# Table slices in PSUM as operands of VectorE's products, and the second power made in halves

## The chip, the cores and the metric

The kernel runs on one core of a Trainium2 chip. The metric is the device time of one execution in microseconds, the median of three runs. An execution has five engines at work beside each other: TensorE (PE in the profile), VectorE (DVE), ScalarE (ACT), GpSimd (POOL) and SyncE (SP), which issues the transfers here. Semaphores order them.

## What is computed

A state space kernel gives the tokens, and a transformer layer follows (attention of 32 heads with a causal mask, and a gated feed-forward part with quantised weights). Only the first stage, the state space kernel and the layer norm behind it, is touched by the change:

```
dt = exp(log_dt); A = -exp(inv_A_real) + 1j * A_imag          # (H=128, N=64)
dtA = A * dt[:, None]
Cc = (B * C) * (exp(dtA) - 1) / A                             # (16, 128, 64)
V = exp(dtA[:, :, None] * arange(1024))                       # (128, 64, 1024)
h = 2 * einsum('chn,hnl->chl', Cc, V).real                    # (16, 128, 1024)
h = h + attention(layernorm(h)); h = h + ffn(layernorm(h))
```

## The kernel before

`ssm_and_norm` makes h and its layer norm. The power exp(dtA l) is never made for all l at once: l is written as 128 i + 16 j + m (i and j below 8, m below 16), and small tables hold the powers of each part, `tab1` for the real part and `tab2` for the imaginary part (with rows 64 to 127 of the partitions arranged for the other component), 32 entries a channel. Columns 0 to 7 of a channel (i) go, rotated by the coefficients, into `a1` and `a2`; columns 8 to 15 (j) and 16 to 31 (m) are multiplied out to the 128 powers of a channel.

The 128 channels go in 16 units (`UNITS`) of 8 channels (`UH`). For a unit u:

- GpSimd multiplies `tab1` slices out to `v` (L238), then `a1` by `c_re` to the first factor `w[s][0]` (L241), then channels 0 to 2 (`CUT` is 3) of `a2` by `c_im` (L242).
- VectorE makes channels 3 to 7 of that last product (`second_factor`, L459), multiplies the `tab2` slices out to `v_second`, a tile of two PSUM banks (`second_power`, L465), and adds it to `v` (`power`, L469).
- TensorE multiplies `v` by the two factors, four channels to a half (`product(u, 0)` and `product(u, 1)`, L258), and ScalarE brings each half out (`columns`, L315). TensorE transposes it to tokens (`to_tokens`, L267), ScalarE copies them out with their total (`tokens`, L323) and SP writes them to the chip's memory (L168).
- The layer norm follows: VectorE's `mean` (L475), ScalarE's `squares` (L331) and `deviation` (L336), VectorE's `inverse` (L481), ScalarE's `normalise` (L340, L342), TensorE's `to_features` (L275), ScalarE's `high` (L346) and VectorE's `low` (L485).

`v`, `w`, `tok` and `nrm` have two buffers each, `v_second`, `pt` and `pn` one. Every engine runs a loop over k that is written out by hand and takes the steps of different units in a fixed order; `each(lag, k)` says whether unit k - lag exists. VectorE's turn k is: second_factor(k + 1), inverse(k - 2), second_power(k + 1), power(k + 1), low(k - 3), then in turns 1 to 6 one step of `rotations` of the second half of the channels, in turns 7 to 10 a quarter of the search for the largest of the next stage's first weights (L650), in turn 13 `find_scale` (L658 and on), mean(k - 1), and in turns 14 and 15 `first.low`. ScalarE's turn is high(k - 3), normalise(k - 2), columns(k, 0), tokens(k - 1), columns(k, 1), squares(k - 1), deviation(k - 1), and in turns 13 and 14 `first.high`. TensorE's is product(k, 0), to_tokens(k - 1), product(k, 1), to_features(k - 2). Behind the token write of unit 10 SP sends the largest weight out and back to all partitions (`exchange`: two small transfers, wv_bigs and wv_all, the second waits for the first). A barrier of all engines ends the stage.

The semaphore `s_v` counts the units whose power is done; `s_mm` counts halves of products; `s_wd`, `s_wp` and `s_v1` say that VectorE's factor, GpSimd's factors and GpSimd's power are ready.

Of the kernel before, what the change touches and what calls it, by code (L numbers as in the profile page):

```python
# [15 lines left out]
P = 128  # L16
# [69 lines left out]
def ssm_and_norm(nc, ssm, cr, ci, h0_dram, xn_hi, xn_lo, ident, w_first, wv_first, b_first, first, rooms):  # L86
# [9 lines left out]
    with ExitStack() as st:  # L96
# [31 lines left out]
        with ExitStack() as tables_only:  # L128
            phase_ps = [tables_only.enter_context(nc.psum_tensor(f"phase_ps{k}", [P, HALF_H, TAB], F32)) for k in two]
        ps = [st.enter_context(nc.psum_tensor(f"ssm_ps{s}", [P, UH // 2, P], F32)) for s in two]  # L130
        v_second = st.enter_context(nc.psum_tensor("v_second", [P, UH * P], F32))
# [6 lines left out]
        s_v1, s_v, s_wp, s_wd, s_mm, s_tr, s_tok, s_mean, s_sq, s_std, s_rs, s_nrm, s_trn, s_hi, s_lo = (  # L138
            sem("a_" + n) for n in ("v1", "v", "wp", "wd", "mm", "tr", "tok", "mean", "sq", "std", "rs", "nrm", "trn", "hi", "lo"))
# [106 lines left out]
        def _(pe):  # L246
            def product(u, part):
                s = u % 2
                if part == 0:
                    pe.wait_ge(s_v, u + 1)  # L250
                    pe.wait_ge(s_wp, u + 1)
                    pe.wait_ge(s_wd, u + 1)
                if u:
                    pe.wait_ge(s_ev[part], u)
                for h in range(UH // 2):
                    cols = slice((part * UH // 2 + h) * P, (part * UH // 2 + h + 1) * P)
                    for k in two:
                        last = nc.tensor.matmul(ps[part][:, h, :], v[s][:, cols], w[s][k][:, cols], start=(k == 0), stop=(k == 1))  # L258
                last.then_inc(s_mm, 1)
# [29 lines left out]
        def _(act):  # L289
# [59 lines left out]
            for k in range(UNITS + 3):  # L349
                if k == UNITS:  # L350
                    tokens(k - 1)
                if each(3, k):
                    high(k - 3)
                if each(2, k):
                    normalise(k - 2)
                if each(0, k):
                    columns(k, 0)
                if each(1, k) and k < UNITS:
                    tokens(k - 1)
                if each(0, k):  # L360
                    columns(k, 1)
                if each(1, k):
                    squares(k - 1)
                    deviation(k - 1)
                if k in (UNITS - 3, UNITS - 2):
                    act.wait_ge(s_v, UNITS // 2)
                    first.high(nc, act, 0, k - UNITS + 3)

        @block.vector
        def _(dve):  # L370
# [83 lines left out]

            def second_factor(u):
                s, hs = u % 2, channels(u, CUT, UH)
                if u >= 2:
                    dve.wait_ge(s_mm, 2 * (u - 1))
                tt(four(w[s][1], C)[:, CUT:UH], bc(a2[:, hs, :], C, 3), bc(cim[:, hs, :], KT, 2), ALU.mult).then_inc(s_wd, 1)  # L459

            def second_power(u):
                ch = channels(u)
                if u:
                    dve.wait_ge(s_v, u)
                chain.after(tt(four(v_second[:], TJ), bc(tab2[:, ch, TI:2 * TI], TJ, 3), bc(tab2[:, ch, 2 * TI:TAB], TI, 2), ALU.mult))  # L465

            def power(u):
                dve.wait_ge(s_v1, u + 1)
                tt(v[u % 2], v[u % 2], v_second[:], ALU.add).then_inc(s_v, 1)  # L469
# [17 lines left out]

            for k in range(-1, UNITS + 3):
                if each(-1, k):
                    second_factor(k + 1)  # L490
                if each(2, k):
                    inverse(k - 2)
                if each(-1, k):
                    second_power(k + 1)
                    power(k + 1)
                if each(3, k):
                    low(k - 3)
                if 1 <= k < 7:
                    rotations(1, k - 1)
                if 7 <= k < 11:  # L500
                    first.find_big_quarter(nc, dve, chain, 0, k - 7)
                if k == UNITS - 3:
                    first.find_scale(nc, dve, chain, 0)
                if each(1, k):
# [2165 lines left out]
```

## Time and profile before

| | |
|---|---|
| median of 3 runs | 1905.37 us (1904.93 to 1909.08) |
| profiled execution | 1913.66 us, span 1911.9 us |
| TensorE, busy share of the span | 93% (1787.0 us) |
| VectorE | 70% (1335.3 us) |
| GpSimd | 52% (992.7 us) |
| ScalarE | 39% (749.7 us) |
| granted TensorE clock, mean | 0.990 |

The profile is one execution of its own, and its times are compared with its own span. In its rows a line number is that of the kernel above, an arrow leads from what is read to what is written, x16 is a count, and a time in brackets is how long the engine stood idle before it, with what released it. Tiles that lie in the room of others go by the name of the room: `v` is shown as magnitude, `w` as phase, `tab1` as w_qk and `tab2` as w_v.

### The profile page before, as it was taken

How to read it: one execution, taken by the hardware profiler on the slowest of the kernel's cores; microseconds unless marked ns; L12 is line 12 of the kernel's file. 1: busy time of each engine (PE TensorE's matmuls, PEld its weight loads, DVE VectorE, ACT ScalarE, POOL GpSimd, SP SyncE). 2: the span in 40 equal slices, each digit the busy share in tenths (PEclk: the TensorE clock that was granted, in tenths of full speed). 3: DMA queues.
4: the chain of work that ended last, by engine and by line, in shares of the span. 5: the costliest groups of instructions: out<-in, count | busy, mean ns of one | idle time of the engine just before them, and what ended most of it. 6: DMA issues, size and time to landing. Idle time of an engine off the chain costs nothing.

```text
span 1911.9 us, 31551 instructions
## 1 busy us (share of the span) xinstructions
PE 1787.0 (93%) x12772; PEld 975.9 (51%) x12772; DVE 1335.3 (70%) x1695; ACT 749.7 (39%) x1072; POOL 992.7 (52%) x675
## 2 busy tenths in 40 slices
PE   0577899999999999999999999999999999999999
PEld 0576566666666656554555344444444444444444
DVE  8996477877788888865555877775665555367775
ACT  4478143433434345431212554544544443112221
POOL 6973043433434333442261366765577776377672
PEclk9998899999999999999999999999999999999999
DMA  2122202111021221126541333333455453533531
GB/s 98 36 75 68 61 15 60 40 37 39 18 88 62 62 75 62 34 99 225 168 138 64 103 113 118 117 115 119 157 155 195 150 170 121 198 131 117 193 114 67
DMA packets 102704, 194.92 MB, mean 102 GB/s; under 512 B 14304, under 2 KB 75488, under 8 KB 92064
## 3 DMA queue, kind: packets, MB, share of 16 engines
q1 hardware_dynamic: 102560, 192.90, 31.4%
q8 instruction: 102, 1.67, 0.4%
q14 instruction: 42, 0.34, 0.1%
HBM read 135.72 MB, written 56.11 MB: 100 GB/s over the span
## 4 chain that ended last, share of the span: by engine, by line
PE 74%; DVE 9%; POOL 2%; issue 2%; ACT 2%; DMA 1%; SPq 0%; DVEq 0%; ACTq 0%
PE acc L1481 13%; PE acc L1483 12%; PE acc L1649 9%; PE acc L1614 4%; PE ps_p L1273 4%; PE ps_p L1275 4%; PE ps_p L1274 4%; PE ps_t L1300 3%; PE acc L1387 3%; PE acc L1388 3%; PE acc L1389 3%; PE ps_p L1289 2%; PE ps_p L1291 2%; PE ps_p L1290 2%; PE ps_l L1490 2%
## 5 line engine op out<-in xcount | busy, mean ns | idle before, releaser
L1127 POOL TENSOR_TENSOR prob<-prob,mx 128x1024 f32<-128x1024 f32 x64 | 121.4, 1897 | 379.8 <-DVE mx L2078 379.8
L1273 PE MATMUL ps_p<-x_hi,w_qk 128*128 128x512 f16 x512 | 194.7, 380 | 0.0
L1274 PE MATMUL ps_p<-x_lo,w_qk 128*128 128x512 f16 x512 | 194.0, 379 | 0.0
L1275 PE MATMUL ps_p<-x_hi,w_qk 128*128 128x512 f16 x512 | 194.0, 379 | 0.0
L1180 POOL TENSOR_TENSOR hidden<-up,hidden 128x512 f16<-128x512 f32 x80 | 91.0, 1159 | 144.3 <-ACT hidden L1907 144.0
L1289 PE MATMUL ps_p<-w_v,x_hi 128*128 128x256 f16 x512 | 142.3, 278 | 7.2 <-PEq L825 3.6
L1132 POOL TENSOR_TENSOR prob<-prob,sm 128x1024 f32<-128x1024 f32 x64 | 120.1, 1896 | 52.9 <-DVE sm L2085 52.9
L1290 PE MATMUL ps_p<-w_v,x_hi 128*128 128x256 f16 x512 | 142.2, 278 | 0.0
L1291 PE MATMUL ps_p<-w_v,x_lo 128*128 128x256 f16 x512 | 142.2, 278 | 0.0
L1741 ACT ACTIVATE pth<-ps_t 128x512 f16<-128x512 f32 x128 | 76.1, 595 | 163.7 <-PE ps_t L1300 163.7
L2330 DVE SCALAR_TENSOR_TENSOR up<-acc,gu_scale,up 128x512 f32<-128x512 f32 x120 | 90.0, 750 | 61.1 <-PE acc L1483 60.0
L258 PE MATMUL ssm_ps<-phase,magnitude 128*128 128x128 f32 x512 | 69.1, 294 | 65.3 <-DVE magnitude L469 62.1
L2330 DVE SCALAR_TENSOR_TENSOR gate<-acc,gu_scale,gate 128x512 f32<-128x512 f32 x120 | 89.7, 747 | 56.2 <-PE acc L1483 55.4
L1481 PE MATMUL acc<-x_hi,q_sums 128*128 128x512 f16 x320 | 121.7, 380 | 1.1 <-issue 0.8
L1481 PE MATMUL acc<-x_sum,q_sums 128*128 128x512 f16 x320 | 121.3, 379 | 0.0
L1483 PE MATMUL acc<-x_sum,q_sums 128*128 128x512 f16 x320 | 121.3, 379 | 0.0
L1483 PE MATMUL acc<-x_lo,q_f 128*128 128x512 f16 x320 | 121.3, 379 | 0.0
L1481 PE MATMUL acc<-x_hi,q_f 128*128 128x512 f16 x320 | 121.3, 379 | 0.0
L1483 PE MATMUL acc<-x_lo,q_sums 128*128 128x512 f16 x320 | 121.3, 379 | 0.0
L2089 DVE SCALAR_TENSOR_TENSOR ptl<-ps_t,pth 128x512 f16<-128x512 f32 x128 | 87.7, 685 | 47.3 <-ACT pth L1741 46.8
L1899 ACT ACTIVATE gate<-gate 128x512 f32<-128x512 f32 (+1 forms) x88 | 55.1, 626 | 135.8 <-DVE gate L2330 133.2
L258 PEld LDWEIGHTS ssm_ps<-phase,magnitude 128*128 128x128 f32 x512 | 66.1, 209 | 65.8 <-DVE magnitude L469 62.3
(386 smaller groups left out, 4598.0 us busy)
## 6 DMA issues: line engine op xcount, KB each, us to landing
q_raw<-in_gu_q SPq DMA_DIRECT2D x42, 1024.0 KB, 6.3
hid_parts<-hidden_parts SPq DMA_DIRECT2D x16, 1376.0 KB, 6.8
hidden_parts<-hidden SPq DMA_DIRECT2D x42, 512.0 KB, 3.5
down_raw<-in_down_q SPq DMA_DIRECT2D x22, 512.0 KB, 3.6
w_raw<-in_w_qk SPq DMA_DIRECT2D x8, 1024.0 KB, 4.8
h_tokens<-n_tok SPq DMA_DIRECT2D x16, 512.0 KB, 3.7
o_parts<-ot SPq DMA_DIRECT2D x32, 256.0 KB, 2.3
wv_raw<-in_w_o SPq DMA_DIRECT2D x8, 1024.0 KB, 4.9
```

The costliest lines, as they stand in the source:

```text
L258: last = nc.tensor.matmul(ps[part][:, h, :], v[s][:, cols], w[s][k][:, cols], start=(k == 0), stop=(k == 1))
L1127: nc.gpsimd.tensor_tensor(prob[s % 2][p][:], prob[s % 2][p][:], bc(mx[p][:], H, 2), ALU.subtract).then_inc(s_sub[p], 1)
L1273: nc.tensor.matmul(out[:], w[:, j % 2, m, 0, at], xn_hi[:, k, tok], start=(k == 0), stop=False)
L1274: nc.tensor.matmul(out[:], w[:, j % 2, m, 0, at], xn_lo[:, k, tok], start=False, stop=False)
L1275: last = nc.tensor.matmul(out[:], w[:, j % 2, m, 1, at], xn_hi[:, k, tok], start=False, stop=(k == KT - 1))
L1289: nc.tensor.matmul(out, xn_hi[:, k, tok], wv[:, g % 2, 0, at], start=(k == 0), stop=False)
L1290: nc.tensor.matmul(out, xn_hi[:, k, tok], wv[:, g % 2, 1, at], start=False, stop=False)
L1291: last = nc.tensor.matmul(out, xn_lo[:, k, tok], wv[:, g % 2, 0, at], start=False, stop=(k == KT - 1))
L1481: nc.tensor.matmul(banks[bank], lev[:, k * P:(k + 1) * P], hi[:, k, :], start=(k == 0 and not adds), stop=False, skip_group_check=adds)
L1483: last = nc.tensor.matmul(banks[bank], lev[:, k * P:(k + 1) * P], lo[:, k, :], start=False, stop=(k == KH - 1), skip_group_check=adds)
L1649: last = nc.tensor.matmul(banks[bank], of_hid(i, part), of_levels(i), start=(not adds and i == 0 and part == 0), stop=(ends and i == KD - ...
L2330: stt(to[:], banks[bank], scl[:, m, i:i + 1], to[:], ALU.mult, ALU.add).then_inc(s_read, 1)
```

## The change

A new PSUM tile `cuts` holds, for two units, the `tab2` slice of columns 8 to 15 of all eight channels and the `a2` slice of channels 3 to 7. The new `slices(u)` copies both with two TENSOR_SCALAR calls (times 1.0) on VectorE, for unit 0 ahead of the loop and for unit k + 2 in turn k. `second_factor` and `second_power` read these copies in place of the tables in SBUF. `second_power` and `power` are made in two parts of four channels, and `v_second` is half as large, so that one bank serves both parts. VectorE's turn k is now: second_factor(k + 1), second_power(k + 1, 0), inverse(k - 2), power(k + 1, 0), low(k - 3), second_power(k + 1, 1), the rotation, slices(k + 2), the quarter or find_scale, power(k + 1, 1), mean(k - 1). `s_v` counts parts, and TensorE waits for the part that it multiplies. The other inputs of the two products (`cim` and columns 16 to 31 of `tab2`) stay in SBUF, as do all operands of GpSimd.

```diff
--- before.py
+++ after.py
@@ -128,15 +128,16 @@
         with ExitStack() as tables_only:
             phase_ps = [tables_only.enter_context(nc.psum_tensor(f"phase_ps{k}", [P, HALF_H, TAB], F32)) for k in two]
         ps = [st.enter_context(nc.psum_tensor(f"ssm_ps{s}", [P, UH // 2, P], F32)) for s in two]
-        v_second = st.enter_context(nc.psum_tensor("v_second", [P, UH * P], F32))
+        v_second = st.enter_context(nc.psum_tensor("v_second", [P, UH // 2 * P], F32))
+        cuts = st.enter_context(nc.psum_tensor("cuts", [P, 2, 2 * UH, TI], F32))
         pt = st.enter_context(nc.psum_tensor("n_pt", [P, KT, P], F32))
         pn = st.enter_context(nc.psum_tensor("n_pn", [P, KT, P], F32))
 
         s_in, s_c, s_const, s_dve, s_re, s_im, s_expm, s_square, s_pool, s_ab, s_turn = (
             sem("a_" + n) for n in ("in", "c", "const", "dve", "re", "im", "expm", "square", "pool", "ab", "turn"))
         s_mag, s_phase, s_trig, s_tab, s_a = (sem("a_" + n) for n in ("mag", "phase", "trig", "tab", "a"))
-        s_v1, s_v, s_wp, s_wd, s_mm, s_tr, s_tok, s_mean, s_sq, s_std, s_rs, s_nrm, s_trn, s_hi, s_lo = (
-            sem("a_" + n) for n in ("v1", "v", "wp", "wd", "mm", "tr", "tok", "mean", "sq", "std", "rs", "nrm", "trn", "hi", "lo"))
+        s_v1, s_v, s_wp, s_wd, s_mm, s_tr, s_tok, s_mean, s_sq, s_std, s_rs, s_nrm, s_trn, s_hi, s_lo, s_cut = (
+            sem("a_" + n) for n in ("v1", "v", "wp", "wd", "mm", "tr", "tok", "mean", "sq", "std", "rs", "nrm", "trn", "hi", "lo", "cut"))
         s_out, s_ev = ([sem(f"a_{n}{s}") for s in two] for n in ("out", "ev"))
         logdt, inva, aim, br, bi = (par[:, k, :] for k in range(5))
         nc.all_engine_barrier()
@@ -246,8 +247,8 @@
         def _(pe):
             def product(u, part):
                 s = u % 2
+                pe.wait_ge(s_v, 2 * u + part + 1)
                 if part == 0:
-                    pe.wait_ge(s_v, u + 1)
                     pe.wait_ge(s_wp, u + 1)
                     pe.wait_ge(s_wd, u + 1)
                 if u:
@@ -363,7 +364,7 @@
                     squares(k - 1)
                     deviation(k - 1)
                 if k in (UNITS - 3, UNITS - 2):
-                    act.wait_ge(s_v, UNITS // 2)
+                    act.wait_ge(s_v, UNITS)
                     first.high(nc, act, 0, k - UNITS + 3)
 
         @block.vector
@@ -452,21 +453,38 @@
             dve.wait_ge(s_tab, 2)
             dve.wait_ge(s_c, 32)
 
+            def slices(u):
+
+                s, ch, hs = u % 2, channels(u), channels(u, CUT, UH)
+                if u >= 2:
+                    dve.wait_ge(s_v, 2 * (u - 1))
+                    dve.wait_ge(s_wd, u - 1)
+                ts(cuts[:, s, 0:UH, :], tab2[:, ch, TI:2 * TI], 1.0, None, ALU.mult).then_inc(s_cut, 1)
+                ts(cuts[:, s, UH + CUT:2 * UH, :], a2[:, hs, :], 1.0, None, ALU.mult).then_inc(s_cut, 1)
+
             def second_factor(u):
                 s, hs = u % 2, channels(u, CUT, UH)
+                dve.wait_ge(s_cut, 2 * (u + 1))
                 if u >= 2:
                     dve.wait_ge(s_mm, 2 * (u - 1))
-                tt(four(w[s][1], C)[:, CUT:UH], bc(a2[:, hs, :], C, 3), bc(cim[:, hs, :], KT, 2), ALU.mult).then_inc(s_wd, 1)
-
-            def second_power(u):
-                ch = channels(u)
-                if u:
-                    dve.wait_ge(s_v, u)
-                chain.after(tt(four(v_second[:], TJ), bc(tab2[:, ch, TI:2 * TI], TJ, 3), bc(tab2[:, ch, 2 * TI:TAB], TI, 2), ALU.mult))
-
-            def power(u):
+                tt(four(w[s][1], C)[:, CUT:UH], bc(cuts[:, s, UH + CUT:2 * UH, :], C, 3), bc(cim[:, hs, :], KT, 2),
+                   ALU.mult).then_inc(s_wd, 1)
+
+            def second_power(u, part):
+
+                mine = slice(part * UH // 2, (part + 1) * UH // 2)
+                ch = channels(u, part * UH // 2, (part + 1) * UH // 2)
+                if u or part:
+                    dve.wait_ge(s_v, 2 * u + part)
+                return chain.mark(tt(v_second[:].rearrange("p (h a b) -> p h a b", h=UH // 2, b=TJ), bc(cuts[:, u % 2, mine, :], TJ, 3),
+                                     bc(tab2[:, ch, 2 * TI:TAB], TI, 2), ALU.mult))
+
+            def power(u, part, made):
+
+                cols = slice(part * UH // 2 * P, (part + 1) * UH // 2 * P)
                 dve.wait_ge(s_v1, u + 1)
-                tt(v[u % 2], v[u % 2], v_second[:], ALU.add).then_inc(s_v, 1)
+                dve.wait_ge(s_dve, made)
+                tt(v[u % 2][:, cols], v[u % 2][:, cols], v_second[:], ALU.add).then_inc(s_v, 1)
 
             def mean(u):
                 dve.wait_ge(s_tok, u + 1)
@@ -485,22 +503,29 @@
                 tt(xn_lo[:].rearrange("p k (c h) -> p k c h", h=H)[:, :, :, channels(u)], pn[:].rearrange("p k (c h) -> p k c h", h=UH),
                    xn_hi[:].rearrange("p k (c h) -> p k c h", h=H)[:, :, :, channels(u)], ALU.subtract).then_inc(s_lo, 1)
 
+            slices(0)
             for k in range(-1, UNITS + 3):
                 if each(-1, k):
                     second_factor(k + 1)
+                    made = second_power(k + 1, 0)
                 if each(2, k):
                     inverse(k - 2)
                 if each(-1, k):
-                    second_power(k + 1)
-                    power(k + 1)
+                    power(k + 1, 0, made)
                 if each(3, k):
                     low(k - 3)
+                if each(-1, k):
+                    made = second_power(k + 1, 1)
                 if 1 <= k < 7:
                     rotations(1, k - 1)
+                if each(-2, k):
+                    slices(k + 2)
                 if 7 <= k < 11:
                     first.find_big_quarter(nc, dve, chain, 0, k - 7)
                 if k == UNITS - 3:
                     first.find_scale(nc, dve, chain, 0)
+                if each(-1, k):
+                    power(k + 1, 1, made)
                 if each(1, k):
                     mean(k - 1)
                 if k in (UNITS - 2, UNITS - 1):
```

## Rows read from the trace of the kernel before

**Rows 1.** Chain that ended last, from its start: start us, us, what.
```profile
194.30 2.30 DVE w_big L2040
```

**Rows 2.** Timeline, VectorE's means of units 0, 5, 11, 14: start us, us, engine, line.
```profile
74.16 0.14 DVE L475 TENSOR_SCALAR n_mean<-n_total 128x1 f32<-128x1 f32 x1
...
111.67 0.15 DVE L475 TENSOR_SCALAR n_mean<-n_total 128x1 f32<-128x1 f32 x1
...
154.38 0.15 DVE L475 TENSOR_SCALAR n_mean<-n_total 128x1 f32<-128x1 f32 x1 [0.63 <-ACT n_tok L323]
...
177.87 0.15 DVE L475 TENSOR_SCALAR n_mean<-n_total 128x1 f32<-128x1 f32 x1 [2.88 <-ACT n_tok L323]
```

**Rows 3.** Grouped lines of VectorE, first stage from 57 us: busy us, mean ns.
```profile
L465 DVE TENSOR_TENSOR v_second<-w_v 128x1024 f32<-128x1024 f32 x16 | 34.3, 2142 | 0.0
L459 DVE TENSOR_TENSOR phase<-a,c_im 128x640 f32<-128x640 f32 x16 | 27.7, 1728 | 0.6 <-PE ssm_ps L258 0.5
```

**Rows 4.** Single lines: shortest, median and longest of one (ns), first and last start.
```profile
L459 DVE TENSOR_TENSOR phase<-a,c_im x16: 816/1926/2581, 57.1 to 163.3; 128x640 f32<-128x640 f32 x16
...
L465 DVE TENSOR_TENSOR v_second<-w_v x16: 1215/1842/2962, 57.8 to 165.8; 128x1024 f32<-128x1024 f32 x16
...
L469 DVE TENSOR_TENSOR magnitude<-magnitude,v_second x16: 1220/1221/1222, 60.8 to 167.6; 128x1024 f32<-128x1024 f32 x16
...
L241 POOL TENSOR_TENSOR phase<-a,c_re x16: 1920/2510/2930, 57.1 to 163.2; 128x1024 f32<-128x1024 f32 x16
```

**Rows 5.** Timeline, VectorE beside GpSimd (POOL), 96 to 99 us.
```profile
96.09 2.38 POOL L241 TENSOR_TENSOR phase<-a,c_re 128x1024 f32<-128x1024 f32 x1
...
96.61 0.14 DVE L475 TENSOR_SCALAR n_mean<-n_total 128x1 f32<-128x1 f32 x1
96.67 2.48 DVE L459 TENSOR_TENSOR phase<-a,c_im 128x640 f32<-128x640 f32 x1
```

**Rows 6.** Timeline of ScalarE, one unit from 127 us; idle time in brackets.
```profile
127.08 1.15 ACT L331 ACTIVATE magnitude<-n_tok,n_mean 128x1024 f32<-128x1024 f32 x1 [1.85 <-DVE n_mean L475]
...
128.56 1.00 ACT L346 ACTIVATE x_hi<-n_pn 128x1024 f16<-128x1024 f32 x1
...
132.40 0.59 ACT L315 ACTIVATE n_xt<-ssm_ps 128x512 f32<-128x512 f32 x1
```

**Rows 7.** Timeline of TensorE, half of a product.
```profile
127.31 1.95 PE L258 MATMUL ssm_ps<-phase,magnitude 128*128 128x128 f32 x16
```

**Rows 8.** Grouped lines of VectorE before 57 us, shapes kept apart.
```profile
L404 DVE TENSOR_SCALAR w_qk<-phase_ps 128x2048 f32<-128x2048 f32 x2 | 4.6, 2291 | 0.1
...
L381 DVE TENSOR_SCALAR n_nrm<-ssm_par 128x256 f32<-128x256 f32 x1 | 0.3, 294 | 1.2 <-DMA ssm_par<-in_ssm 1.2
```

**Rows 9.** Timeline, first unit of the loop, all engines.
```profile
57.11 2.56 POOL L241 TENSOR_TENSOR phase<-a,c_re 128x1024 f32<-128x1024 f32 x1 [3.48 <-DVE a L443]
...
59.63 1.82 POOL L242 TENSOR_TENSOR phase<-a,c_im 128x384 f32<-128x384 f32 x1
...
62.07 1.22 PE L258 MATMUL ssm_ps<-phase,magnitude 128*128 128x128 f32 x4 [62.07 <-DVE magnitude L469]
```

**Rows 10.** Timeline around the exchange of the largest weight, all engines and SP's queue.
```profile
146.49 0.20 ACT L323 ACTIVATION_READ_ACCUMULATOR n_tok<-n_pt 128x1 f32 x1
...
147.28 0.59 SPq L628 DMA_DIRECT2D wv_bigs<-wv_big  x1
...
155.79 0.33 SPq L630 DMA_DIRECT2D wv_all<-wv_bigs  x1
...
161.04 0.28 DVE L658 TENSOR_REDUCE wv_pow<-wv_all 128x1 f32<-128x128 f32 x1
...
161.28 1.92 POOL L238 TENSOR_TENSOR magnitude<-w_qk 128x1024 f32<-128x1024 f32 x1
...
162.12 1.11 DVE L660 TENSOR_SCALAR bv_scaled<-b_qkv,wv_scale 128x2 f32<-128x2 f32 x1
```

**Rows 11.** DMA issues, 60 to 200 us: count, KB each, median us to landing.
```profile
wv_all<-wv_bigs SPq DMA_DIRECT2D x1, 64.0 KB, 4.5
```

## The prediction

> **What bounds the kernel now.** I read the page's shares first (TensorE is busy 93% of the span, but the stage around the change is the first tenth), then the chain of work that ended last, from its beginning. The chain opens at 194 us with the reduction of the next stage's weights [rows 1]: it stands behind the barrier that ends the first stage and waits for nothing that has a clock of its own. So whatever the first stage ends earlier, the kernel ends earlier by the same amount. Next I read the timeline of the first stage, unit by unit. VectorE's `mean` (L475) occurs once in a unit: from unit 0 at 74.16 to unit 14 at 177.87 [rows 2] are 14 periods, 7.41 us each. What fills a period? The grouped lines give `second_factor` (L459) a mean of 1728 ns and `second_power` (L465) 2142 ns [rows 3]; one operation's own spread gives their shortest as 816 and 1215 ns, while `power` (L469), of the same 1024 elements as L465 but with one operand in PSUM, never left 1220 to 1222 ns [rows 4]. The reader is to see that spread: the same work takes up to 2962 ns. The timeline of VectorE beside GpSimd shows why: L459 starts at 96.67, while GpSimd works from 96.09 to 98.47, and ends at 99.15, 0.68 us after GpSimd's end, which is the time that its 640 elements take [rows 5]. With both operands in SBUF, whoever comes second stands still until the other is done. The excess over the shortest is 0.91 us and 0.93 us a unit, 29.4 us over 16 units [rows 3, 4]. ScalarE sees it as waits for the mean, as the 1.85 us before its square at 127.08 [rows 6].
>
> **What the stage can fall to.** ScalarE's work of one unit goes from the square at 127.08 to `columns` at 132.40, 5.32 us, plus about 0.5 for that last copy: 5.8 us a unit without the waits [rows 6]. TensorE needs less: two halves of a product of 1.95 [rows 7] and two sets of eight transposes, half as many instructions, by that estimate 1.0 each: 5.9, near ScalarE's; the layout below looks at whether the two collide. GpSimd needs 1.92 twice and, for 384 elements at the same rate, 0.83: 4.6 us [rows 4] (the 0.83 is 384 elements at 1.75 to 1.85 ns with some 0.15 fixed, an estimate from L241's shortest, 1920 ns for 1024). So ScalarE is late next, not VectorE's blocked products.
>
> **Price of each part.** From 816 ns for 640 elements and 1220 for 1024 [rows 4] VectorE pays 1.05 ns an element and 0.15 a call; neighbours that wait for nothing start 0.08 before the end of the one in front (96.67 is before 96.61 + 0.14) [rows 5]. (1) `second_factor` reads its table operand from `cuts` in PSUM: 1.73 becomes 0.82, a step of 0.75. (2) `second_power` in halves of 512: 0.68 each, step 0.61, so 1.22 for 2.14. (3) `power` in halves: 1.22 for a step of 1.14, plus 0.08. In the other order the wait of power for second_power goes behind `inverse`, the rotation or the copies. (4) `slices`: two calls of 64 and 40 elements that no row shows. Nearest are a TENSOR_SCALAR of 256 elements from SBUF to SBUF at 294 ns, and 2048 elements out of PSUM at 2291 ns [rows 8]: 0.15 is the lower end; the upper end is 0.2 plus one whole GpSimd operation of 1.92, because L660, a TENSOR_SCALAR of 2 elements, took 1.11 us from 162.12 to 163.23, when the GpSimd operation of 161.28 ended [rows 10]. I take 0.2 each, 0.25 in steps for both: 256 elements in 294 ns are half a nanosecond each, two a cycle, and that form could be what blocked; 2048 out of PSUM run at 1.05 ns, so an operand in PSUM gives up the double rate, and `cuts` is one. (5) The waits on s_cut, s_v and s_wd name work that VectorE finished before in its own order; they cost nothing while that order holds. Were a copy late, `inverse`, the products and `low` would stand behind `second_factor` on VectorE, and ScalarE's `normalise` would wait for them; the copies are made a whole unit ahead, so five other VectorE steps lie between. (6) TensorE's wait moves from the whole power to its half: product(u, 0) may start one half earlier, which no engine waits for once ScalarE is the bound. (7) One bank less for v_second and one for the copies: no time, unless a PSUM operand read with repeats is slower. Lower bound 1.05 ns an element as in L469, upper twice that; I take the lower, as L465's repeats out of SBUF cost nothing in its shortest run [rows 4].
>
> The Trainium skill, page SBUF — State Buffer, section Who interferes with whom, says that `tensor_scalar` can take the two-port mode and then is fully blocked by GpSimd; this speaks against the copies, and would make each cost as much as the upper end; by that rule L660 agrees [rows 10]. Its page VectorE: DVE Perf Modes, section Mode 2×_2P, says that this mode requires SBUF, which would leave them at 0.2; the two rates agree [rows 8]. No row of before has the mixed form, SBUF in and PSUM out.
>
> **One period laid out**, with the mean at 0. ScalarE squares at 0.2, starts `high` at 1.7 and ends it at 2.7 (128.56 is 1.48 after 127.08, for 1.0) [rows 6]. VectorE: factor and first half done by 1.45, `inverse` at 1.8 behind the deviation (ScalarE's call in front of `high`), first power to 2.5, `low` from 2.7 on, its 1024 elements a step of 1.14, to 3.85, second half to 4.45, copies to 4.7, power to 5.3: mean possible at 5.3, but ScalarE's total is there only at 5.6 (`columns` starts 5.32 behind the square) and its next square follows at 6.0, so the period is 5.8. TensorE: `to_features` from the end of `normalise` at 4.1, product(k + 1, 0) to 7.0, the transposes to tokens, product(k + 1, 1) to 9.7, which is 3.7 of the next period; `columns` of the first half is wanted at 10.0, three after its product. TensorE holds up nobody, and starts GpSimd's next unit at 3.7. With a rotation or a quarter of the maximum (0.7) the mean comes at 6.0: period 6.0. A rotation still has two SBUF operands and meets GpSimd's first product of that unit: it is held up to 1.1 us in one period and less in the next, 0.5 on the mean: 6.5.
>
> **The sum.** Head: GpSimd's operations of 2.56 and 1.82 at 57.11 and 59.63 [rows 9] become 1.92 and 0.83, ready at 59.9; VectorE has copied and made its half by 59.6; the first product starts at 60.0, not 62.07 [rows 9]. Unit 1 is then GpSimd's 4.6 later, 64.5 (first part 59.9 + 1.9, and so on); unit 2's first power waits for GpSimd at 66.3, and behind it come a half, a rotation held to 68.7, the copies and a power: mean(0) at 69.7, not 74.16: −4.4. Means 0 to 5, with rotations: 6.5 each for 37.5 now: −5.0. Means 5 to 11: four with quarters at 6.0, 0.4 for what follows the last of them, two at 5.8, against 42.7: −6.6. Means 11 to 14: `find_scale` adds 2.2 (161.04 to 163.23), and must wait. SP waits from 147.28 to 155.79 for its first small transfer before it issues the second, which lands in 4.5, at 160.3; the reduction that needs it starts at 161.04 without idling [rows 10, 11]. SP's issue follows the total of unit 10 at 146.7 [rows 10], and the change shortens nothing in this: it lands 13.6 after that total, which in the new layout is at mean(10), while VectorE asks for it 5.8 + 4.7 = 10.5 after. It stalls for 3, and power(14, 1) and mean(12) stand behind it, the square and product(14, 1) behind those: 13.6 + 2.2 + 0.6 for the power − 5.8 = 10.5 for this period. The two up to mean 14 take 6.8 each, with 1.0 on ScalarE for `first.high`, 1024 elements as in `high`. 24.1 for 23.5 now [rows 2]: +0.6. What follows mean(14) is a chain of single steps that the change doesn't touch: 0. Together −15.4. The profiled execution took 1913.66 with a span of 1911.9; its span should become 1896.5. The median of the runs is 8.3 lower, 1905.4, and loses the same: 1890.0.
>
> **The rivals.** *The copies are held like L660.* Each would wait as L459 and L465 do, 0.92 on the mean, 1.85 a unit: 15 units are 28, less 4 that the shorter periods can absorb: 24 − 15 = +9, so 1914; at a full GpSimd operation each, 3.8 a unit, 1935 or so. It decides from 1.3 us of holding a unit. For it: 1.11 us at 162.12 [rows 10]; against it the rate out of PSUM. (This is the rule of the Trainium skill's SBUF — State Buffer cited above.) *PSUM read with repeats at half rate.* 640 elements and twice 512 cost 1.73 more a unit, of which 0.5 hides under the deviation and `high`: 1.2 times 15, less 4 of cover, is +14 on −15: 1904, no change. Against it: 16 runs of L469 at full rate. *The gain is smaller:* rotations held a whole 1.1 each time (+3), periods of 6.2 as engines hand over with less slack than laid out (+3 to +5), lower TensorE clock in more stretches: 1896 to 1900. *The gain is larger:* the small transfer lands in half the 8.5 us, so that find_scale doesn't stall (−3), and rotations fall clear (−2): 1884.
>
> **How the numbers follow.** The forecast's case has 0.68, larger gain 0.05, smaller gain 0.12, no change by slow PSUM reads 0.06, held copies 0.09. A change of 0.2% is 3.8 us, about what this measurement can tell from none. Faster is 0.68 + 0.05 + 0.12 = 0.85, same 0.06, slower 0.09. The forecast's own range is 1884 to 1895: rotations 2.5 either way, the stalled transfer 3. The smaller gain is taken in: 1883 to 1900, and the last two cases stay out.
>
> **What would show it.** L459 near 0.82 and all halves near 0.68, with hardly a spread; L238 to L242 at their shortest but where a rotation runs; the copies near 0.2. ScalarE's waits for the mean under 0.3 in the plain periods, and `low` idle before it, waiting for ScalarE. Means 5.8 to 6.5 apart; a VectorE wait of 3 before find_scale's first reduction; the next stage's weight reduction at 179 instead of 194.3. Copies over 0.3 on the mean, a product half over 0.8, or periods over 7 outside find_scale's would prove the price or the layout wrong; if the periods shrink and the end doesn't, it is the rigid shift that fails.

## The result, and the profile after

The changed kernel takes 1891.1 us (median of four runs, 1889.9 to 1892.3) beside 1905.3 for the kernel before (1904.9 to 1909.1): ratio 0.9919, 95% interval 0.9907 to 0.9931. The forecast was 1890.0, in a range of 1883 to 1900.

The profiled execution's span is 1890.5, 21.4 less than before, while the medians differ by 14.2. So the stage itself has to be looked at. The chain that ended last begins as before with the next stage's weight reduction (start us, us, what):

```profile
178.85 2.30 DVE w_big L2065
...
184.67 6.32 DMA w_every<-w_bigs
```

It begins at 178.85, where [rows 1] has 194.30: the first stage is 15.45 us shorter, against a forecast of 15.4. The other 6 us of the span lie behind it. The chain of the kernel before has 8.03 us for its w_every transfer where this one has 6.32, and in the two stretches of 10 us that begin 10 us behind that start the granted clock is 0.79 and 0.86 there, 1.00 here. Over all the profiles of this study the time from this reduction to the end lies between 1709.7 and 1717.6 us, and the two that have a w_every of 7.5 us and more are the longest of them. These 6 us were not forecast, and no run assigns them to the change.

The clock differs within the stage too, but doesn't explain the shorter stage. In the profile before, the stretches from 111.74 to 119.20 and from 147.68 to 155.02 had a granted clock of 0.81 and 0.77; they lasted 7.46 and 7.34 us, where the mean period is 7.41. After, it is 1.00 from unit 0's mean to unit 14's.

The grouped lines of VectorE in the stage after (busy us, mean ns), to be read beside [rows 3]:

```profile
L479 DVE TENSOR_TENSOR v_second<-cuts,w_v 128x512 f32<-128x512 f32 x32 | 22.1, 690 | 0.1
...
L470 DVE TENSOR_TENSOR phase<-cuts,c_im 128x640 f32<-128x640 f32 x16 | 13.1, 816 | 1.0 <-PE ssm_ps L259 1.0
L462 DVE TENSOR_SCALAR cuts<-w_v 128x64 f32<-128x64 f32 x16 | 3.5, 220 | 0.1
...
L463 DVE TENSOR_SCALAR cuts<-a 128x40 f32<-128x40 f32 x16 | 3.1, 192 | 0.0
```

The single lines, shortest, median and longest in ns, beside [rows 4]:

```profile
L470 DVE TENSOR_TENSOR phase<-cuts,c_im x16: 807/814/826, 57.2 to 149.0; 128x640 f32<-128x640 f32 x16
...
L479 DVE TENSOR_TENSOR v_second<-cuts,w_v x32: 681/690/699, 57.9 to 153.8; 128x512 f32<-128x512 f32 x32
...
L242 POOL TENSOR_TENSOR phase<-a,c_re x16: 1920/1932/2433, 56.9 to 145.7; 128x1024 f32<-128x1024 f32 x16
```

The 16 factor products (L470, before L459) now lie between 807 and 826 ns; their mean went from 1728 to 816. The 32 halves of the second power (L479) lie between 681 and 699; two of them with their mean of 690 make 1.38 where the whole took 2.14. The spread is gone, and with it the hold on the other side: GpSimd's median for L242 (before L241) is 1932 where it was 2510 [rows 4]. The copies take 0.22 and 0.19, and all 32 of them start while a GpSimd instruction runs.

One period of VectorE, between the means of units 6 and 7 (L499 is `inverse`, L503 `low`, L675 a quarter):

```profile
109.76 0.15 DVE L493 TENSOR_SCALAR n_mean<-n_total 128x1 f32<-128x1 f32 x1
109.82 0.81 DVE L470 TENSOR_TENSOR phase<-cuts,c_im 128x640 f32<-128x640 f32 x1
110.56 0.69 DVE L479 TENSOR_TENSOR v_second<-cuts,w_v 128x512 f32<-128x512 f32 x1
111.54 0.16 DVE L499 RECIPROCAL n_rs<-n_std 128x1 f32<-128x1 f32 x1 [0.30 <-ACT n_std L337]
111.62 0.69 DVE L487 TENSOR_TENSOR magnitude<-magnitude,v_second 128x512 f32<-128x512 f32 x1
112.45 1.22 DVE L503 TENSOR_TENSOR x_lo<-n_pn,x_hi 128x1024 f16<-128x1024 f32 x1
113.60 0.69 DVE L479 TENSOR_TENSOR v_second<-cuts,w_v 128x512 f32<-128x512 f32 x1
114.19 0.21 DVE L462 TENSOR_SCALAR cuts<-w_v 128x64 f32<-128x64 f32 x1
114.32 0.19 DVE L463 TENSOR_SCALAR cuts<-a 128x40 f32<-128x40 f32 x1
114.42 0.67 DVE L675 TENSOR_REDUCE wv_quarters<-wv_raw 128x1 f32<-128x512 f32 x1
115.13 0.69 DVE L487 TENSOR_TENSOR magnitude<-magnitude,v_second 128x512 f32<-128x512 f32 x1
115.73 0.14 DVE L493 TENSOR_SCALAR n_mean<-n_total 128x1 f32<-128x1 f32 x1
```

In starts, with the mean at 0, that is inverse at 1.8, low at 2.7, second half at 3.8, copies at 4.4, power at 5.4, the next mean at 5.97: the forecast's layout for a period with a quarter, to a tenth.

The means of units 0, 5, 11, 12 and 14 after, beside [rows 2]:

```profile
70.77 0.14 DVE L493 TENSOR_SCALAR n_mean<-n_total 128x1 f32<-128x1 f32 x1
...
103.79 0.15 DVE L493 TENSOR_SCALAR n_mean<-n_total 128x1 f32<-128x1 f32 x1
...
139.52 0.15 DVE L493 TENSOR_SCALAR n_mean<-n_total 128x1 f32<-128x1 f32 x1 [0.30 <-ACT n_tok L324]
...
148.97 0.14 DVE L493 TENSOR_SCALAR n_mean<-n_total 128x1 f32<-128x1 f32 x1
...
162.47 0.15 DVE L493 TENSOR_SCALAR n_mean<-n_total 128x1 f32<-128x1 f32 x1 [1.72 <-ACT n_tok L324]
```

The stage split at these means, in us:

| stretch | before | forecast | after |
|---|---|---|---|
| mean of unit 0, at | 74.16 | 69.7 | 70.77 |
| means 0 to 5 (rotations) | 37.5 | 32.5 | 33.0 |
| means 5 to 11 (quarters, then plain) | 42.7 | 36.1 | 35.7 |
| means 11 to 14 (`find_scale`, `first.high`) | 23.5 | 24.1 | 22.95 |
| mean 14 to the next stage | 16.4 | 16.4 | 16.4 |

Two waits that were forecast are there. A rotation runs into GpSimd's product, VectorE and GpSimd side by side:

```profile
94.46 1.93 POOL L239 TENSOR_TENSOR magnitude<-w_qk 128x1024 f32<-128x1024 f32 x1 [2.18 <-PE ssm_ps L259]
...
94.86 2.07 DVE L442 TENSOR_TENSOR a_tmp<-ssm_t,w_v 128x512 f32<-128x512 f32 x1
```

L442, 512 elements, takes 2.07 us and ends 0.54 us behind GpSimd's L239 (94.46 + 1.93 = 96.39): that period lasts 7.4, and the one before, whose rotation (L440) took 0.68, lasts 5.85. And `find_scale` waits for the small transfer:

```profile
144.24 0.19 DVE L463 TENSOR_SCALAR cuts<-a 128x40 f32<-128x40 f32 x1
146.87 0.29 DVE L683 TENSOR_REDUCE wv_pow<-wv_all 128x1 f32<-128x128 f32 x1 [2.44 <-DMA wv_all<-wv_bigs]
```

It waits 2.44 us; the forecast had 3.

### The profile page after: what moved, and what is told of

The parts are those of the page before. It is cut to its first block, busy times and chain, and to the rows that moved or that the text cites. A ratio compares the mean times of both kernels' runs of the same rounds, so it can differ in the third digit from the quotient of the medians.

```text
span 1890.5 us, 31673 instructions
## 1 busy us (share of the span) xinstructions
PE 1778.7 (94%) x12772; PEld 968.5 (51%) x12772; DVE 1312.4 (69%) x1759; ACT 748.3 (40%) x1072; POOL 974.0 (52%) x675
## 4 chain that ended last, share of the span: by engine, by line
PE 75%; DVE 9%; POOL 2%; issue 2%; ACT 2%; DMA 1%; DVEq 0%; ACTq 0%
PE acc L1506 13%; PE acc L1508 13%; PE acc L1674 9%; PE acc L1639 4%; PE ps_p L1298 4%; PE ps_p L1300 4%; PE ps_p L1299 4%; PE acc L1412 3%; PE acc L1414 3%; PE acc L1413 3%; PE ps_t L1325 3%; PE ps_p L1314 2%; PE ps_p L1316 2%; PE ps_p L1315 2%; PE ps_l L1515 2%
## 5 line engine op out<-in xcount | busy, mean ns | idle before, releaser
L259 PE MATMUL ssm_ps<-phase,magnitude 128*128 128x128 f32 x512 | 64.3, 281 | 62.1 <-POOL phase L243 59.7
L1760 ACT ACTIVATE prob<-prob 128x1024 f32<-128x1024 f32 x64 | 67.6, 1057 | 79.8 <-POOL prob L1152 79.8
```

## Experiments

The runs came in three groups, each beside runs of the kernel before on its own chip (medians 1909.2, 1908.4 and 1909.3). The ratio is always that to the kernel before, and where runs of different groups are compared the ratios count, since the kernel before took 1905.3 us in the comparison above and 3 to 4 more in these groups. The start of the next stage's reduction ("reduction at") is from the run's own profile; a stage is called longer or shorter by it.

### Where the copies lie

```diff
-        cuts = st.enter_context(nc.psum_tensor("cuts", [P, 2, 2 * UH, TI], F32))
+        cuts = sb("cuts", [P, 2, 2 * UH, TI])
```

> The changed kernel with one difference: the tile of copies lies in SBUF and no longer in PSUM; instructions, order and waits are the same. Theory (VectorE and GpSimd hold each other wherever VectorE reads two SBUF operands): the factor product goes back to 1.7 us on the mean (0.82 shortest), the halves of the second power to about 1.3 (0.69 shortest), and the two copies, now SBUF to SBUF, are held as well, up to 0.9 each on the mean; the next stage's first reduction starts at 195 to 215 us and the kernel takes 1905 to 1925. Rival (the gain is the new order and the split in halves, wherever the operands lie): reduction at 179, 1891 us, no spread in the product's durations.

Measured: 1926.2, ratio 1.0089 (1.0073 to 1.0105), slower than the kernel before, reduction at 212.93. VectorE and GpSimd in one period of this run:

```profile
136.45 1.92 POOL L239 TENSOR_TENSOR magnitude<-w_qk 128x1024 f32<-128x1024 f32 x1 [2.90 <-PE ssm_ps L259]
...
137.92 1.00 DVE L479 TENSOR_TENSOR v_second<-cuts,w_v 128x512 f32<-128x512 f32 x1
...
138.33 2.37 POOL L242 TENSOR_TENSOR phase<-a,c_re 128x1024 f32<-128x1024 f32 x1
...
138.84 1.92 DVE L462 TENSOR_SCALAR cuts<-w_v 128x64 f32<-128x64 f32 x1
```

and its single lines:

```profile
L462 DVE TENSOR_SCALAR cuts<-w_v x16: 195/1369/1923, 57.6 to 179.4; 128x64 f32<-128x64 f32 x16
...
L463 DVE TENSOR_SCALAR cuts<-a x16: 171/172/1915, 57.7 to 181.2; 128x40 f32<-128x40 f32 x16
```

The copy of 64 elements starts at 138.84, 0.51 behind the start of GpSimd's L242, and ends at 140.76, 0.06 behind its end: 1.92 us for 64 elements. The half before it is held too, by L239 until 138.37: 1.00 for 0.69. The same instructions in the same order lose 34.1 us of the stage when nothing but the tile's place changes. So the gain comes from the place, and the forecast's rival of the held copies describes this kernel, not the changed one. The time lies 1.2 above the expected range. The theory was less exact on who pays: the factor product had a mean of 922 ns (1.7 expected), the halves 1059 (1.3), the larger copy 1278 (1.1 at most), the smaller 389. A hold falls on whoever meets a GpSimd instruction in its turn, and in this order that is mostly the larger copy.

### The halves without the copies

```diff
-            slices(0)
-                if each(-2, k):
-                    slices(k + 2)
-                dve.wait_ge(s_cut, 2 * (u + 1))
-... bc(cuts[:, s, UH + CUT:2 * UH, :], C, 3) ...
+... bc(a2[:, hs, :], C, 3) ...
-... bc(cuts[:, u % 2, mine, :], TJ, 3) ...
+... bc(tab2[:, ch, TI:2 * TI], TJ, 3) ...
```

> The changed kernel without the copies: halves, order and waits of the change, but both products of VectorE read the tables in SBUF directly. Theory: every product is held by GpSimd as in the kernel before, and there are three of them in a unit where there were two, so the stage ends at 190 to 200 us and the kernel takes 1902 to 1912. Rival (halves and order bring the gain by themselves, as power no longer waits right behind second_power and a product starts a half earlier): 1891 to 1895.

Measured: 1911.2, ratio 1.0010 (1.0000 to 1.0021), reduction at 199.08. The order and the split bring nothing by themselves; they cost 4.8 us of the stage. They pay for the room: the copies lie in PSUM that v_second gives up by being made in halves.

### Factor and second power one at a time

The factor from SBUF alone, then the second power alone; the other operand still comes from `cuts`:

```diff
-... bc(cuts[:, s, UH + CUT:2 * UH, :], C, 3) ...
+... bc(a2[:, hs, :], C, 3) ...
```

> The changed kernel, but the factor product reads its table in SBUF (both copies still made). Theory: L470 goes from 0.82 back to 1.5 to 1.9 us on the mean and stands at the front of VectorE's turn, where 0.3 us of it are covered by the wait for the deviation: 0.4 to 0.8 a unit on the way to the mean, reduction at 185 to 190 us, 1897 to 1902. Rival (ScalarE covers it all): 179, 1891.

```diff
-... bc(cuts[:, u % 2, mine, :], TJ, 3) ...
+... bc(tab2[:, ch, TI:2 * TI], TJ, 3) ...
```

> The changed kernel, but both halves of the second power read their table in SBUF (the factor product still reads the copy). Theory: each half is held separately, 0.69 becomes 1.1 to 1.6, the second of them fully on the way to the mean: 0.8 to 1.2 a unit, reduction at 189 to 195 us, 1901 to 1907; together with the run that takes the factor from SBUF the losses add to that of the run with halves alone, within 4 us. Rival (ScalarE covers it all): 179, 1891.

Measured: 1898.4, ratio 0.9949 (0.9935 to 0.9963), reduction at 186.47; and 1904.7, ratio 0.9975 (0.9965 to 0.9985), reduction at 190.99. The held line of each (grouped lines, mean ns):

```profile
L470 DVE TENSOR_TENSOR phase<-a,c_im 128x640 f32<-128x640 f32 x16 | 25.0, 1563 | 0.0
```

```profile
L479 DVE TENSOR_TENSOR v_second<-w_v 128x512 f32<-128x512 f32 x32 | 34.7, 1085 | 0.1
```

With the factor in SBUF the stage is 7.6 us longer than that of the changed kernel, with the second power in SBUF 12.1; together 19.8, and the run with both in SBUF is 20.2 longer (199.08 - 178.85) although it also saves the copies. Both parts count, and nearly add. One more hold sits in these numbers: at the end of the last quarter a SCALAR_TENSOR_TENSOR of one element (L678, `wv_big` out of `wv_big` and `b_top`, all in SBUF) took 1.92 us in the first of the two runs, 0.76 in the second and 0.98 (L674) in the run with halves alone, where the changed kernel has 0.30. Some 1.6 of the 7.6 us so lie in this one hold and not in the factor product, and that the two losses add so closely is in part chance.

### Who sets the period now

One more ScalarE copy of 512 elements a unit, to a scratch tile of its own in SBUF (its lines, and those of the semaphore, are left out here and below):

```diff
+                if part == 1:
+                    if u:
+                        act.wait_ge(s_more, u)
+                    nc.scalar.activation(scratch[:].rearrange("p (m h) -> p m h", h=UH // 2), ps[1][:].rearrange("p h m -> p m h"), ACT.Copy).then_inc(s_more, 1)
```

> The changed kernel with one more ScalarE copy of 512 elements in each unit, from the product's second half to a scratch tile (0.59 us, 0.5 as a step), in front of the real copy. Theory (ScalarE is the bound in the plain periods and 0.15 off it in those with a quarter): periods of 5.80 become 6.3, those of 5.97 become 6.3 too, the 9.45 of find_scale stays; reduction at 182.5 to 185 us, 1895 to 1897. Rival (TensorE or VectorE is the bound, and ScalarE has room): 179 to 180.

Measured: 1895.7, ratio 0.9934 (0.9921 to 0.9947), reduction at 182.62. Four of its means, a period with a quarter and a plain one:

```profile
116.56 0.15 DVE L499 TENSOR_SCALAR n_mean<-n_total 128x1 f32<-128x1 f32 x1
...
122.85 0.15 DVE L499 TENSOR_SCALAR n_mean<-n_total 128x1 f32<-128x1 f32 x1
...
136.75 0.15 DVE L499 TENSOR_SCALAR n_mean<-n_total 128x1 f32<-128x1 f32 x1 [0.30 <-ACT n_tok L330]
...
143.03 0.15 DVE L499 TENSOR_SCALAR n_mean<-n_total 128x1 f32<-128x1 f32 x1 [0.30 <-ACT n_tok L330]
```

6.29 with a quarter, where the changed kernel has 5.97, and 6.28 plain, where it has 5.80: as expected. That the whole stage met its expectation too (3.8 us longer) is partly luck. The periods with a rotation hardly grew, while the one from 122.85 to 131.12 lasts 8.27 (6.38 in the changed kernel), mostly through a hold:

```profile
128.65 1.93 POOL L244 TENSOR_TENSOR phase<-a,c_re 128x1024 f32<-128x1024 f32 x1
...
128.72 1.88 DVE L684 SCALAR_TENSOR_TENSOR wv_big<-wv_big,b_top 128x1 f32<-128x1 f32 x1
```

L684, the L678 of the changed kernel, handles one element. It starts 0.07 behind GpSimd's instruction and ends with it: 1.88 us for the 0.30 of the changed kernel. All that it reads and writes lies in SBUF.

One more VectorE product of 512 elements a unit:

```diff
                     made = second_power(k + 1, 1)
+                    if k + 1:
+                        dve.wait_ge(s_more, k + 1)
+                    tt(scratch[:].rearrange("p (h a b) -> p h a b", h=UH // 2, b=TJ), bc(cuts[:, (k + 1) % 2, 0:UH // 2, :], TJ, 3),
+                       bc(tab2[:, channels(k + 1, 0, UH // 2), 2 * TI:TAB], TI, 2), ALU.mult).then_inc(s_more, 1)
```

> The changed kernel with one more product of 512 elements on VectorE in each unit, from the copies in PSUM and the table to a scratch tile in SBUF (0.69 us, 0.6 as a step), behind the second half of the second power. Theory (VectorE has 0.4 to 0.5 of room in a plain period and none in one with a rotation or a quarter): plain periods go from 5.80 to 5.8 to 6.0, those with a quarter from 5.97 to 6.55, those with a rotation by 0.6 too or less where the hold shifts; find_scale's wait absorbs its own: reduction at 183 to 186 us, 1895 to 1898. Rival (ScalarE alone is the bound): every period stays, reduction at 179.

Measured: 1899.6, ratio 0.9955 (0.9940 to 0.9970), reduction at 188.18. A period with a quarter and a plain one:

```profile
116.51 0.15 DVE L495 TENSOR_SCALAR n_mean<-n_total 128x1 f32<-128x1 f32 x1
...
123.08 0.15 DVE L495 TENSOR_SCALAR n_mean<-n_total 128x1 f32<-128x1 f32 x1
...
143.17 0.15 DVE L495 TENSOR_SCALAR n_mean<-n_total 128x1 f32<-128x1 f32 x1
...
149.03 0.15 DVE L495 TENSOR_SCALAR n_mean<-n_total 128x1 f32<-128x1 f32 x1
```

6.57 with a quarter (5.97 in the changed kernel) and 5.86 plain (5.80). So in a plain period VectorE has some 0.55 us of room and ScalarE none, and in one with a quarter VectorE's order is the path: the extra 0.6 appears whole. The stage lost 9.3 us where 4 to 7 were expected; the rest came in the head (mean 0 at 73.05) and in periods with a rotation.

### The wait of find_scale

```diff
-                if u == UNITS - 6:
+                if u == UNITS - 7:
                     first.exchange(sp, 0)
-                if 7 <= k < 11:
-                    first.find_big_quarter(nc, dve, chain, 0, k - 7)
+                if 6 <= k < 10:
+                    first.find_big_quarter(nc, dve, chain, 0, k - 6)
```

> The changed kernel with the four quarter searches one turn earlier (turns 6 to 9) and the exchange of the largest weight behind the token write of unit 9 in place of 10; find_scale stays in turn 13. Theory: the 2.44 us that find_scale waits for the small transfers go, and nothing else changes but for turn 6, which now has a rotation and a quarter: reduction at 176.5 to 177.5 us for 178.85, 1889 us, a gain of 1.5 to 2.4. Rival (the wait was covered by ScalarE's or TensorE's later work): reduction stays at 178.5 to 179.

Measured: 1889.1, ratio 0.9900 (0.9887 to 0.9913), reduction at 177.96. The reduction that needs the transfer no longer idles:

```profile
L683 DVE TENSOR_REDUCE wv_pow<-wv_all 128x1 f32<-128x128 f32 x1 | 0.3, 276 | 0.0
```

The period of find_scale fell from 9.45 to 6.77, 2.7 us. Only 0.9 arrived, less than the 1.4 to 2.4 that the stage was expected to give: the turn with both a rotation and a quarter took back 0.7, and mean 0 came 1.2 later, most of it because TensorE's first 48 matmuls took 8.52 us in this execution and 7.59 in the other, where the edit has no part. The stage shows that the wait is gone; a gain of the whole kernel is not shown, since the interval of its ratio overlaps that of the changed kernel (0.9907 to 0.9931).

### Rotations and quarters out of GpSimd's way

```diff
                     power(k + 1, 0, made)
+                if 0 <= k < 6:
+                    rotations(1, k)
+                if 6 <= k < 10:
+                    first.find_big_quarter(nc, dve, chain, 0, k - 6)
                 if each(3, k):
                     low(k - 3)
-                if 1 <= k < 7:
-                    rotations(1, k - 1)
```

(with the exchange behind unit 9, as above)

> As the run with the earlier exchange, and in addition the rotations (turns 0 to 5) and the quarters (6 to 9) stand behind the first half of power and in front of low, where VectorE waits for ScalarE and GpSimd is idle. Theory (VectorE's order and GpSimd's holding of the rotations make periods of 5.97 and 6.0 to 7.5 out of ScalarE's 5.8): all periods before find_scale go to 5.8 to 5.95, reduction at 172.5 to 174.5 us, 1884 to 1887. Rival (those periods are set by TensorE or GpSimd): reduction at 176.5, 1889.

Measured: 1886.6, ratio 0.9885 (0.9871 to 0.9900), reduction at 172.38. Its means of units 5 to 7:

```profile
101.69 0.15 DVE L493 TENSOR_SCALAR n_mean<-n_total 128x1 f32<-128x1 f32 x1
...
107.49 0.15 DVE L493 TENSOR_SCALAR n_mean<-n_total 128x1 f32<-128x1 f32 x1
...
113.29 0.15 DVE L493 TENSOR_SCALAR n_mean<-n_total 128x1 f32<-128x1 f32 x1
```

5.80 each with a quarter in them, ScalarE's floor; the other two with a quarter last 5.74 and 6.12, the four with a rotation 6.35, 5.80, 6.21 and 6.03, and four of these six lie above the 5.95 that was expected at most. This beats both kernels: its interval lies below that of the changed kernel. The stage is 6.5 us shorter than the changed kernel's, and the two ratios differ by 0.0034, which is 6.5 us too. Against the run with only the earlier exchange the stage is 5.6 shorter but the median only 2.5, and those two intervals overlap; in this profile the w_every transfer behind the stage took 7.55.

### The small product of mean and inverse deviation on VectorE

```diff
-                nc.vector.reciprocal(rs[u % 2][:, 0:1], std[u % 2][:]).then_inc(s_rs, 1)
+                chain.after(nc.vector.reciprocal(rs[u % 2][:, 0:1], std[u % 2][:]))
+                tt(rs[u % 2][:, 1:2], minus_mean[u % 2][:], rs[u % 2][:, 0:1], ALU.mult).then_inc(s_rs, 1)
-                nc.scalar.activation(rs[u % 2][:, 1:2], minus_mean[u % 2][:], ACT.Copy, scale=rs[u % 2][:, 0:1]).then_inc(s_turn, 1)
-                act.wait_ge(s_turn, u + 1)
```

> As the run with everything moved, and the small product of mean and inverse deviation (128x1, 0.28 us on ScalarE) is made by VectorE behind its reciprocal. Theory (ScalarE is the bound, VectorE has slack): the period falls by 0.2 to 0.32 to about 5.55, 14 units and the tail: reduction 3 to 4.5 us earlier than in the run without it, 1881 to 1883. Rival (the loop through mean, square, deviation, inverse and low sets the period whoever makes the product): no change or 0.1 a unit longer, for the 0.2 us on VectorE.

Measured: 1891.1, ratio 0.9911 (0.9898 to 0.9925), reduction at 180.13: a stage 7.75 us longer than without it and a median 4.5 higher, and neither theory had it. The timeline shows the cause at its largest:

```profile
94.26 1.94 POOL L242 TENSOR_TENSOR phase<-a,c_re 128x1024 f32<-128x1024 f32 x1
94.32 0.16 DVE L497 RECIPROCAL n_rs<-n_std 128x1 f32<-128x1 f32 x1 [0.59 <-ACT n_std L337]
94.52 1.69 DVE L498 TENSOR_TENSOR n_rs<-n_mean,n_rs 128x1 f32<-128x1 f32 x1
...
96.14 0.85 POOL L243 TENSOR_TENSOR phase<-a,c_im 128x384 f32<-128x384 f32 x1
```

A product of one element a partition (L498) takes 1.69 us, because both its inputs lie in SBUF and GpSimd's L242 had started 0.26 before. The 16 calls take 0.16 to 1.69; what they take above 0.16 adds up to 5.3 us. `find_scale`'s L684, the L660 of [rows 10], took 1.78 here for 0.30. The two plain periods in which the product is hardly held (0.20 and 0.28) fall to 5.31 and 5.33, and in the first of them TensorE is busy for all 5.31.

The same with a form that reads one tensor and a scalar:

```diff
-                tt(rs[u % 2][:, 1:2], minus_mean[u % 2][:], rs[u % 2][:, 0:1], ALU.mult).then_inc(s_rs, 1)
+                ts(rs[u % 2][:, 1:2], minus_mean[u % 2][:], rs[u % 2][:, 0:1], None, ALU.mult).then_inc(s_rs, 1)
```

> As the run with everything moved and the small product on VectorE, but that product is a TENSOR_SCALAR (mean times a per-partition scalar) and no longer a TENSOR_TENSOR with two SBUF operands. Theory (in the run before it the 128x1 product was held by GpSimd, up to 1.69 us for one element, because it had two SBUF operands; without the hold the period is 5.31 us, where TensorE is busy without a gap): the call takes 0.15 to 0.2 each time, periods are 5.3 to 5.45, the next stage's first reduction starts at 166 to 169 us (172.4 in the run with everything moved), and the kernel takes 1880 to 1884. Rival (a scalar operand read from SBUF is held just as well): the call takes 0.15 to 1.7, reduction near 180, 1891.

Its line:

```profile
L498 DVE TENSOR_SCALAR n_rs<-n_mean,n_rs x16: 214/214/217, 75.3 to 164.2; 128x1 f32<-128x1 f32 x16
```

Measured: 1885.4, ratio 0.9877 (0.9860 to 0.9893), reduction at 172.04. The call is never held: 214 to 217 ns, 16 times, and 13 of them start while a GpSimd instruction runs. Nothing but the form of this call differs from the run before, and the stage is 8.1 us shorter: that is the price of the hold with all that it shifts. The period is another matter: 5.3 to 5.5 in the plain ones as expected, but 5.98 to 6.3 in the eight with a rotation or a quarter, 49.1 us together where the run without this product has 47.9. There TensorE waits 4.5 us for `low`, which stands behind the rotation or the quarter in VectorE's order (3.2 in the run without this product), and ScalarE waits 4.0 us for the mean, in seven of them (1.1 in one). With ScalarE shorter, VectorE's order is the path again. The stage came out level with the run before the last (172.04 for 172.38), 3 to 6 us short of the expectation, and the medians of the two, taken on different chips, don't tell them apart.

## Why the prediction was right, step by step

**The shift.** The stage's end moves and what follows moves with it: shown within what an execution varies (1709.7 to 1717.6 from the reduction to the end). The size of the stage's gain, 15.45 for 15.4, is better than the forecast deserves, since four of its terms were off by 0.4 to 1.2 and cancelled.

**The hold.** That VectorE's two-SBUF products and GpSimd stand still for each other was the main argument, and moving one tile between the memories showed it from both sides: 15.45 us gained with the copies in PSUM, 18.6 lost against the kernel before with them in SBUF. The price of each part (0.82, 0.68, 0.2) was met within 0.02.

**The copies.** The forecast took them as free of the hold, with a rival of 0.09 that said otherwise. In PSUM they are free (213 to 228 and 184 to 195 ns); in SBUF the larger one is the most held of all. The upper end of that rival was summed wrongly: 3.8 us in 15 units are 57, less 4 of cover and 15 of gain, which makes 1943 and not 1935. The run with the copies in SBUF, where holds of several instructions count together, took 1926.2. The Trainium skill, SBUF — State Buffer, section Who interferes with whom, lists `tensor_scalar` among the instructions that can be blocked whole: by that rule, the run with the copies in SBUF agrees (1923 ns for 64 elements). The Trainium skill, VectorE: DVE Perf Modes, section Mode 2×_2P, wants SBUF for that mode: the changed kernel agrees, whose copies end in PSUM and were never held.

**PSUM read with repeats** costs what SBUF costs: 816 ns for 640 elements, 690 for 512. That rival is out.

**The bound.** ScalarE at 5.8 in plain periods and VectorE's order at 6.0 in those with a quarter: both shown, the first by the added copy, the second by the added product. The prediction put TensorE at 5.9 and in the same sentence below ScalarE's 5.8. That reading was wrong, and without consequence: the run with the small product as a TENSOR_TENSOR has a plain period of 5.31 in which TensorE is busy throughout, so 5.31 is enough for it and it was not the bound.

**The head** came 1.1 late, as much as means 11 to 14 came early; no other term was off by more. The forecast let GpSimd run from unit to unit without a wait, so that unit 2's part was ready at 66.3. But GpSimd needs `v` back from TensorE, and TensorE was slow at the start:

```profile
59.68 7.59 PE L259 MATMUL ssm_ps<-phase,magnitude 128*128 128x128 f32 x48 [59.68 <-POOL phase L243]
...
65.66 1.93 POOL L239 TENSOR_TENSOR magnitude<-w_qk 128x1024 f32<-128x1024 f32 x1 [1.51 <-PE ssm_ps L259]
```

These are TensorE's first instructions; it stood idle for 59.68 us before them. The first half of the product took 3.79 us, until ScalarE could copy it at 63.47, where a later half takes 1.95, although the profile gives a granted clock of 1.00 there. GpSimd waited 1.51 us, its part was ready at 67.59, and mean 0 came at 70.77, not 69.7. The kernel before has the same slow start: from 62.07 until ScalarE's copy at 65.89. So its trace could have told. Why the start is slow stays open.

**Rotations** took 0.5 more than forecast in all. **Means 11 to 14** came 1.1 shorter than forecast: the small transfer landed 0.4 sooner after unit 10's total (13.2 us for 13.6), and L685, the L660 of [rows 10], took 0.44 where L660 was held and took 1.11.

**Open** stays the difference between 15.45 us of the stage and 14.2 of the medians. The chain behind the stage depends on when two small transfers land (3.3 to 3.8, and 4.0 to 8.0 over all runs), which would cover it; nothing here was made to show it.

## What to carry to other kernels

When VectorE and GpSimd work side by side, look at the spread of one instruction's durations, not at its mean: a shortest that fits its elements and a longest of that plus a GpSimd operation is a hold, and it goes as soon as one of VectorE's inputs lies in PSUM, even if it must be copied there first. Anything moved to VectorE beside a busy GpSimd, down to one element, should have one SBUF input, and the copy itself must not go from SBUF to SBUF. With the hold gone, ask what stands in the slots where the other engine is waited for: here moving the rotations and quarters made the stage 5.6 us shorter, a third of the change again.

## What the runs showed of the hardware that was not expected

A TENSOR_TENSOR of one element a partition was held and took 1.69 us, a SCALAR_TENSOR_TENSOR of one element 1.88 and 1.92, and a TENSOR_SCALAR of two elements 1.78. A TENSOR_SCALAR of one element with a scalar read from SBUF was not held in 16 times (214 to 217 ns). TensorE took 3.79 us for its first half of a product and 1.95 for later ones, with a granted clock of 1.00 in both stretches.
